# First attention: groups of weighted values issued in pairs, in front of every second turn

## The reference, cut to what matters

```python
scores = jnp.einsum('bhid,bhjd->bhij', qh, kh)
rel = jnp.clip(pos[None, :] - pos[:, None], -K, K) + K
bias = jnp.take_along_axis(bias_r, rel, axis=-1)
attn = jax.nn.softmax(scores + bias, axis=-1)
out = jnp.einsum('bhij,bhjd->bhid', attn, vh)
```

## Time and profile before

| what | value |
|---|---|
| median of 3 runs | 5563.9 us |
| the profiled execution | 5562.97 us |
| its span, first to last instruction | 5561.3 us |
| TensorE matmul busy | 5158.7 us (93%) |
| VectorE busy | 4147.2 us (75%) |
| ScalarE busy | 3111.0 us (56%) |
| GpSimd busy | 997.2 us (18%) |
| mean granted TensorE clock | 0.959 |

### The profile page before, as it was taken

One profiled execution on the slowest core, in us unless ns is written; L12 is line 12 of the kernel. 1 busy time (PEld: TensorE's weight loads), 2 busy tenths in 40 slices (PEclk: granted clock), 3 DMA queues, 4 the chain that ended last, 5 costly groups with the idle time before them and its releaser, 6 DMA issues. The chain is left out here.

```text
span 5561.3 us, 115505 instructions
## 1 busy us (share of the span) xinstructions
PE 5158.7 (93%) x34272; PEld 2723.7 (49%) x34272; DVE 4147.2 (75%) x8689; ACT 3111.0 (56%) x4539; POOL 997.2 (18%) x791
## 2 busy tenths in 40 slices
PE   8599999999999999999999999998599989899989
PEld 4233333333333333333333333334488867788866
DVE  6488888888888888888888888871477744677755
ACT  4266666666666666666666666671266532456521
POOL 0211111111111111111111111100233310233211
PEclk9599999999999999999999999995699999999999
DMA  6312212222122122121221211111200000000000
GB/s 202 78 48 54 54 49 55 51 52 56 48 55 53 49 54 54 49 54 48 54 54 48 54 49 49 51 41 33 95 1 0 0 17 0 17 0 0 0 38 23
DMA packets 199753, 248.33 MB, mean 45 GB/s; under 512 B 60718, under 2 KB 128628, under 8 KB 197876
## 3 DMA queue, kind: packets, MB, share of 16 engines
q1 hardware_dynamic: 194532, 226.77, 14.8%
q0 software_dynamic: 5136, 20.45, 2.0%
HBM read 210.73 MB, written 36.18 MB: 44 GB/s over the span
## 5 line engine op out<-in xcount | busy, mean ns | idle before, releaser
L767 DVE TENSOR_REDUCE group_max<-shared_ps 128x1 f32<-128x512 f32 x4096 | 2682.7, 687 | 581.9 <-PE shared_ps L491 476.5
L644 ACT ACTIVATE probs<-scores 128x1024 f32<-128x1024 f32 x2048 | 2012.0, 1021 | 1045.8 <-PE scores L517 667.5
L491 PE MATMUL shared_ps<-keys,max_queries 96*128 96x512 bf16 x4096 | 1434.2, 385 | 2.0 <-issue 1.7
L517 PE MATMUL scores<-queries,keys 98*128 98x512 bf16 (+3 forms) x4096 | 1214.3, 371 | 90.9 <-ACT probs L644 89.8
L532 PE MATMUL out_ps<-probs,values 128*17 128x512 f32 x8192 | 1083.1, 601 | 0.4 <-ACT probs L644 0.4
L491 PEld LDWEIGHTS shared_ps<-keys,max_queries 96*128 96x128 bf16 x4096 | 395.7, 97 | 1116.0 <-DVE group_max L767 506.9
L231 POOL TENSOR_TENSOR near_window<-near_bias,one_f 128x1536 bf16<-128x1536 f32 x128 | 351.4, 2746 | 2912.0 <-DVE max_parts L761 2263.2
L517 PEld LDWEIGHTS scores<-queries,keys 98*128 98x128 bf16 x4096 | 359.3, 98 | 466.5 <-ACT probs L644 241.1
L543 PE MATMUL shared_ps<-block_q,block_table 96*128 96x32 bf16 x4096 | 271.5, 233 | 81.1 <-POOL block_q L428 81.1
L543 PEld LDWEIGHTS shared_ps<-block_q,block_table 96*128 96x128 bf16 x4096 | 231.2, 114 | 187.4 <-issue 138.2
L1190 POOL TENSOR_TENSOR norm<-norm,layer_expo 128x16 f32<-128x16 f32 x64 | 186.2, 2910 | 704.6 <-DVE norm L1576 704.6
(11 more groups left out here) (194 smaller groups left out, 5832.7 us busy)
## 6 DMA issues: line engine op xcount, KB each, us to landing
keys<-k_parts SPq DMA_DIRECT2D x384, 96.0 KB, 2.1
values<-v_wide SPq DMA_DIRECT2D x128, 272.0 KB, 2.7
keys<-k_parts SPq DMA_DIRECT2D x384, 64.0 KB, 2.0
keys<-k_parts SPq DMA_DIRECT2D x128, 132.0 KB, 2.4
k_parts<-part SPq DMA_DIRECT2D x96, 128.0 KB
queries<-q_parts SPq DMA_DIRECT2D x768, 16.0 KB, 1.7
max_queries<-q_parts SPq DMA_DIRECT2D x768, 16.0 KB, 1.7
keys<-k_parts SPq DMA_DIRECT2D x384, 32.0 KB, 1.8
```

The costliest lines, as they stand in the source:

```text
L491: mm = pe.matmul(bank, max_queries[par][:, t * P:(t + 1) * P], keys[par][0:ROWS, (t + TPC * g) * P:(t + TPC * (g + 1)) * P], start=True, s ...
L517: mm = pe.matmul(out[:, 0:cut], keys[par][:, c * P:(c + 1) * P], queries[par][:, 0:cut], start=True, stop=True)
L644: act.activation(probs[s % 4][:], scores[s % 2][:], ACT.Exp).then_inc(exp_done, 1)
L767: dve.tensor_reduce(group_max[par][:, k:k + 1], bank, AX.X, ALU.max).then_inc(max_read, 1)
```

## The change

In front of every even turn TensorE issues two groups of weighted values, pv(t) and pv(t+1); in front of the odd turns none. All else, on every engine, keeps its order.

```diff
                 for turn in range(QUADS):
-                    pv_quad(n, par, turn)
+                    if turn % 2 == 0:
+                        pv_quad(n, par, turn)
+                        pv_quad(n, par, turn + 1)
                     for i in range(4):
                         slot = 4 * turn + i
```

## The result

The changed kernel takes 6127.7 us (median of 6 runs, 6107.19 to 6134.28) beside 5563.1 us for the kernel before (6 runs, 5561.98 to 5565.97): ratio 1.1007, 95% interval 1.0995 to 1.1019. It is 565 us slower, where 394 were forecast, and it lies above the stated range. The profiled execution is the quickest of the six, 6107.19 us with a span of 6105.5.

A forecast was written before the change was run, and what follows sets the result against it. The prediction took TensorE to bound the chunk, except in turn 7, where scores wait for exponentials and VectorE is late. It summed 5563 + 276 (chain) + 118 (clock) = 5957 us, with an 8-in-10 range of 5820 to 6045.

The forecast's parts named there:

- the clock: At chunk ends, more waits make TensorE's clock fall more often: 90 falls at 1.4 us, less 5 at 1.6, +118 us.
- Switches: Turns 0 to 5: fewer changes between full-width and strip matmuls on TensorE, -0.38 us a chunk.
- VectorE behind eight slots: Turns 0 to 5: maxima of slots 12, 15 and 20 wait for VectorE's reductions, +0.42 us a chunk.
- The wait for exponential 15: Front of turn 6: pv(7) waits 1.09 us, slot 24 and all behind it start later, +1.97 us a chunk.
- The wait for exponential 3: Chunk's start: pv(1), right behind pv(0), waits for exponential 3, +0.15 us a chunk.
- Sum of the chain: All terms but the clock: 2.16 us a chunk in 118 chunks, 2.6 in the next eight, together 276 us.
- the clock falls in nearly every chunk: Rival: the chain's 276 us plus clock falls at full price, 195 us, up to 6040 us; chance 0.12.
- The rival of the half-taken shift: Stretch from slot 24 to pv(0) shrinks by up to 0.98 us, leaving +1.15 a chunk, 5713 us; chance 0.07.
- the faster one: Rival: switches saved and nothing waited for, 0.57 us in 126 chunks, 5491 us; chance 0.04.
- 20 falls at 1.6 us: Rival with the clock as it is: the chain's 276 us and up to 20 falls, 5845 us; chance 0.21.
- The reading of the stretch behind slot 24: Slot 24 to next pv(0), 6.66 us: a chain over near adds, exponentials and scores that pv(7)'s leaving does not shorten.

The follow-up runs named there:

- the kernel with its waits filled: Changed kernel plus twelve spare matmuls a chunk: four between pv(6) and pv(7), six before slot 28, two behind slot 29; 5838.0 us.
- The three pairs alone: Changed kernel with pairs before turns 0, 2 and 4 only, pv(6) and pv(7) each before their own turn; 5596.5 us.
- the two attempts at it: Kernel before with only pv(6) and pv(7) paired, before turn 7: 5585.6 us; kernel before with near adds of pairs 0 and 1 one slot earlier: 5573.2 us.
- the same pair: Kernel before with one pair alone, pv(1) and pv(2) in front of turn 1; 5541.8 us, ratio 0.9965.
- eight in the right two places: Changed kernel with spare matmuls only in turn 7's two waits, six before slot 28 and two behind slot 29; 5839.8 us.
- four in the other place: Changed kernel with spare matmuls only between pv(6) and pv(7); 6117.8 us.
- the fourth pair alone: Changed kernel with only pv(6) and pv(7) paired, in front of turn 6, all other groups single; 6154.7 us, ratio 1.1073.

## Why the prediction was wrong

The direction and the mechanism were right; **the term that failed is the clock**, "90 x 1.4 - 5 x 1.6 = +118 us". It measured some 285 us, and the factor that was mis-sized is the price of one fall. Step by step, with averages over the chunks 1 to 116 of the traces, leaving out each stretch that a fall touches:

- *Switches, and VectorE behind eight slots.* Right. In the kernel with its waits filled it is 13.56 us from pv(0) to pv(4) where it was 13.58, -0.02 for a forecast of -0.01 (the wait for exponential 3 is in it). From pv(4) to slot 20 it is 4.66 where it was 4.49, +0.17 for a forecast of +0.20.
- *The wait for exponential 15.* Right to 0.01 us: slot 24 comes 3.48 behind slot 22 in place of 1.51, and behind it nothing gets shorter.
- *The wait for exponential 3.* Forecast 0.15. The chunk shown below has the joined pv(0) and pv(1) at 2.14 us where an undisturbed pair takes 1.91; over all chunks it is 0.15 or 0.22, 0.19 on average.
- *Sum of the chain.* A chunk at full clock takes 29.64 us with the waits filled and 27.52 before, so 2.12 for a forecast of 2.16. In the eight chunks without bias matmuls the extra over the others was put at 0.5 and is 1.0 (28.56 for 25.43), and the last chunk, left at nothing, takes 3.4. In all 276 us forecast, 279 measured; that the two agree so closely is in part luck, as these small errors cancel. The three pairs alone, 24 us by the forecast's terms, measured 37. The eight chunks and the last one make 13 of the 37.
- *The clock.* How often: I took 90 of 127 chunks, a choice for which no row stood. It came out near: 99 falls in the profiled execution. How dear: "Each costs at most the 1.6 us" was taken from falls of half the length. In the changed kernel a fall lasts mostly 6.83 us; it covers the sum, both first groups and the first scores of the next chunk. The profiled executions of the changed kernel and of the one with its waits filled are 271 us apart, which is 2.7 us a fall in place of 1.4. With 2.7 the forecast's own 90 falls would have given 5563 + 276 + 235 = 6074 us. The bound of 1.6 had been read off falls under other conditions, and it should have been doubled for the range at least. Why the low level lasts longer here stays open.

The rival "the clock falls in nearly every chunk", which had 0.12, comes nearest in time, but its count did not come true: 99 falls in 128 chunks lie close to my 90. Its upper value, 6040 us, was too low for the same reason: the price of one fall. In kind the trace agrees with the rule of the Trainium skill that I set beside it ("TensorE: Matmul & The Clock Gate", "A second HAM failure mode: psum-queue depth-cycling"): with short waits between groups of matmuls the clock swung between its two levels 99 times, where it was 5. The rival of the half-taken shift is refuted by the stretch from slot 24 to pv(0), which did not shrink (6.61 us on average for 6.62), and the faster one by the ratio. Two sums of the rivals are loose, without a bearing on the rest: 20 falls at 1.6 us come to 5863 us and not to 5845, and 2.16 less 0.98 is 1.18 and not 1.15.

The reading of the stretch behind slot 24 was good for a shift and too simple for an edit inside it: "VectorE's near adds, exponentials 0 and 1" is only the longest of several nearly equal chains, as the two attempts at it showed.

```profile
991.24 2.14 PE L532 MATMUL out_ps<-probs,values 128*17 128x512 f32 x16
993.31 0.39 PE L491 MATMUL shared_ps<-keys,max_queries 96*128 96x512 bf16 x1
...
1008.97 0.39 PE L503 MATMUL shared_ps<-ident_b,max_parts 128*2 128x128 bf16 x4
1009.50 0.39 PE L491 MATMUL shared_ps<-keys,max_queries 96*128 96x512 bf16 x1
```

These rows of the changed kernel's timeline carry the smaller points: the pair that waits for exponential 3, and `max_to_rows`, now 0.53 us from its start to slot 20 where it was 0.32, for VectorE's bank.

## What to carry to other kernels

When a group of matmuls is moved forward, look up for each wait in it which engine releases it and what that engine does first; a wait that had slack of a turn may have none, and everything queued behind it moves. New waits of TensorE at the end of a loop are paid twice, once as time and once as a lower clock behind them: price the second from a bound that allows longer falls than the ones seen, or test it by filling the waits with spare matmuls. A pair of strip groups gains its 0.2 us only where the second group's operands are long ready and the other engines are covered by other work; where VectorE had no cover the same pair cost 0.75 us.

## What the runs showed of the hardware that was not expected

- Twelve spare matmuls a chunk made the kernel 290 us faster (6127.7 to 5838.0), by keeping TensorE at 2.4 GHz; eight in the right two places did the same (5839.8), four in the other place nothing (6117.8).
- In 128 chunks the clock fell 5 times in the kernel before, 99 times in the changed one, 117 times with the fourth pair alone and never with the waits filled. The longest single wait of TensorE in the changed kernel between 286.4 and 3500 us is 1.4 us.
- A fall of the clock lasted 3.4 us (369.27 to 372.70) in the kernel before and 6.8 us (1019.63 to 1026.46) in the changed one, though TensorE was busy throughout both.
- Groups of strip matmuls follow each other at 0.44 us a wave with nothing lost, also when a wait for a semaphore stands between them that is met already.
